# Stores and refills of the images issued by ScalarE instead of GpSimd in a two-layer spectral kernel

## What is computed

```python
# layer 0 (cut)
f = fft2(x, axes=(1, 2)); Xh = f.real - f.imag          # kept: 23 of the width frequencies
o1 = relu(Xk @ w1[0] + b1[0]);  o2 = o1 @ w2[0] + b2[0]
x = ifft2(softshrink(o2, 0.01)).real + x
# layer 1 (cut)
xf = rfft2(x); xr, xi = xf.real, xf.imag
o1r = relu(xr @ w1[0] - xi @ w1[1] + b1[0]);  o1i = relu(xi @ w1[0] + xr @ w1[1] + b1[1])
o2r, o2i = softshrink(...), softshrink(...)
y = irfft2(o2r + 1j * o2i) + x
```

## Time and profile before

| | us |
|---|---|
| median of 3 runs | 584.18 (583.78 to 585.0) |
| the profiled execution | 583.46 |
| its span | 581.6 |
| PE busy in the span | 528.7 (91%) |
| DVE busy | 302.6 (52%) |
| ACT busy | 217.1 (37%) |
| POOL busy | 123.8 (21%) |
| DMA moved | 104.60 MB, mean 180 GB/s |

### The profile page before, as it was taken

How to read it: one execution, slowest core, us unless ns; L and a number is a source line. 1 busy time by engine, 2 the same in 40 slices (tenths; PEclk the granted TensorE clock), 3 DMA queues, 4 the chain that set the end, 5 groups by cost and what they waited for, 6 DMA issues and landing times.

```text
span 581.6 us, 14177 instructions
## 1 busy us (share of the span) xinstructions
PE 528.7 (91%) x5846; PEld 366.4 (63%) x5846; DVE 302.6 (52%) x668; ACT 217.1 (37%) x487; POOL 123.8 (21%) x135
## 2 busy tenths in 40 slices
PE   4308998999999999999999999999999999989787
PEld 1105677667766677667766777667766777776533
DVE  7102444446763476446753576437744576456522
ACT  2203543553334533543345424443245333433102
POOL 9201122001321034111330033102330122011210
PEclk9758999999999999999999999999999999999969
DMA  8795654457894968765885789686885664353486
GB/s 188 216 231 126 167 134 115 129 130 171 243 260 131 200 183 250 225 158 150 258 238 148 163 220 267 183 180 170 252 242 129 155 184 149 89 116 96 132 214 200
DMA packets 76718, 104.60 MB, mean 180 GB/s; under 512 B 7762, under 2 KB 63304, under 8 KB 76527
## 3 DMA queue, kind: packets, MB, share of 16 engines
q1 hardware_dynamic: 61906, 60.14, 39.9%
q0 software_dynamic: 10608, 40.45, 25.5%
q10 hardware_dynamic: 4140, 3.11, 2.4%
HBM read 52.23 MB, written 51.43 MB: 178 GB/s over the span
## 4 chain that ended last, share of the span: by engine, by line
PE 85%; DMA 4%; DVE 4%; issue 3%; SPq 2%; POOL 1%; ACT 1%; POOLq 0%; DVEq 0%; ACTq 0%
PE ps L632 14%; PE ps L656 12%; PE ps L563 12%; PE ps L532 11%; PE ps L580 11%; PE ps L619 10%; PE ps L596 6%; PE ps L643 5%; PE ps L607 3%; DMA scr_f<-fs 3%; PE ps L567 2%; DVE img L511 1%; DMA bt<-scr_f 1%; SPq L257 1%; DVE ns L493 1%
## 5 line engine op out<-in xcount | busy, mean ns | idle before, releaser
L532 PE MATMUL ps<-img,cst 128*64 128x384 f32 (+1 forms) x368 | 82.9, 523 | 16.1 <-ACT fs L369 8.4
L511 DVE TENSOR_TENSOR img<-ps,img 90x768 f32<-90x768 f32 x90 | 81.4, 905 | 26.0 <-PE ps L563 24.7
L563 PE MATMUL ps<-jr,cst 64*128 64x384 f32 (+1 forms) x368 | 83.8, 523 | 5.5 <-DVE img L511 5.0
L341 POOL TENSOR_TENSOR xs<-xs,nt 128x360 f32<-128x360 f32 (+1 forms) x48 | 41.8, 870 | 219.0 <-ACT xs L378 165.1
L632 PE MATMUL ps<-wt,o 128*109 128x96 f32 (+1 forms) x768 | 85.0, 263 | 1.1 <-DVE o L477 0.3
L632 PEld LDWEIGHTS ps<-wt,o 128*109 128x109 f32 (+1 forms) x768 | 76.3, 171 | 14.5 <-issue 10.0
L580 PE MATMUL ps<-cst,bt 128*64 128x90 f32 x1472 | 68.9, 247 | 17.6 <-DMA bt<-scr_f 17.6
L485 DVE SCALAR_TENSOR_TENSOR ns<-p,ps 109x384 f32<-109x384 f32 x96 | 53.1, 553 | 58.5 <-ACT p L403 58.5
L656 PE MATMUL ps<-ns,cst 64*90 64x192 f32 x736 | 73.6, 330 | 7.7 <-DVE ns L493 7.6
L656 PEld LDWEIGHTS ps<-ns,cst 64*90 64x90 f32 x736 | 59.2, 154 | 32.4 <-issue 30.6
L580 PEld LDWEIGHTS ps<-cst,bt 128*64 128x64 f32 x1472 | 60.2, 139 | 29.6 <-DMA bt<-scr_f 18.0
(11 more groups left out here) (41 smaller groups left out, 415.0 us busy)
## 6 DMA issues: line engine op xcount, KB each, us to landing
y<-img POOLq DMA_DIRECT2D x35, 540.0 KB, 5.0
img<-x POOLq DMA_DIRECT2D x30, 540.0 KB, 7.4
scr_i<-et SPq DMA_DIRECT2D x48, 270.0 KB, 3.5
scr_f<-fs SPq DMA_DIRECT2D x176, 72.0 KB, 3.1
bt<-scr_f SPq DMA_DIRECT2D x40, 270.0 KB, 4.7
jr<-scr_i SPq DMA_DIRECT2D x48, 216.0 KB, 6.3
y<-img SPq DMA_DIRECT2D x11, 270.0 KB, 2.9
img<-x SPq DMA_DIRECT2D x5, 540.0 KB, 8.3
```

Source lines behind the costliest of these rows:

```text
L341: nc.gpsimd.tensor_tensor(re, re, nt[s % 2][:, :, 0:kws(s), 0:H], ALU.subtract).then_inc(re_ok, 1)
L511: nc.vector.tensor_tensor(y, p, y, ALU.add).then_inc(i_add, 1)
L532: last = mm(ps[64 * r:64 * r + 64, P3 + g % 2, 0:(b - a) * HC], K["w_fwd"], img[t % IMGS][:, a:b, :].rearrange("p h c -> p (h c)"), start= ...
L563: last = mm(ps[:, B0 + r, 0:n], K["w_inv"][64 * r:64 * r + 64, :], jr[k][64 * r:64 * r + 64, at, 0:n], start=True, stop=whole)
```

## The change

POOL keeps the clearing of buffers at the start and the subtraction. The stores of y, the refills and the first loads of img2 move into ACT's list, at the same places of `schedule()`'s order; there the first loads of img2 stand ahead of the d0 copy of ACT. A refill now follows the store two chunks later instead of one, and the entry at the head of the next task holds the refills of chunks 4 and 5. The waits for the last stores move from POOL to PE's end.

```diff
 # POOL
-            def refill(t, c):
 ...
-                    if s < NXC:
-                        pool.dma_start(img[2][0:W, r0:r1, :], ...).then_inc(x_ld[2][s], 16)
-                if kind == "inv" and what[0] < TASKS - 1 and (what[1] % 2 == 1 or what[1] == GROUPS - 1):
-                    pool.wait_ge(i_add, t * GROUPS + g + 1)
-                    pool.dma_start(out[...], img[k][0:W, r0:r1, :]).then_inc(y_st[k][c], 16)
-                    if c > 0:
-                        refill(t, c - 1)
-                if kind == "load" and what[0] % STEPS == 2 and what[0] // STEPS >= 2:
-                    refill(what[0] // STEPS - 2, NXC - 1)
 # ACT
+            def refill(t, c):
+                    act.wait_ge(y_st[k][c], 16 * (t // IMGS + 1))
+                    act.dma_start(img[k][0:W, r0:r1, :], x[...]).then_inc(x_ld[k][c], 16)
 ...
+                if kind == "d0" and what[0] < NXC:
+                    act.wait_ge(x_clr[2], 1)
+                    act.dma_start(img[2][0:W, r0:r1, :], ...).then_inc(x_ld[2][s], 16)
+                if kind == "inv" and what[0] < TASKS - 1 and (what[1] % 2 == 1 or what[1] == GROUPS - 1):
+                    act.wait_ge(i_add, t * GROUPS + g + 1)
+                    act.dma_start(out[...], img[k][0:W, r0:r1, :]).then_inc(y_st[k][c], 16)
+                    if c > 1:
+                        refill(t, c - 2)
+                if kind == "load" and what[0] % STEPS == 2 and what[0] // STEPS >= 2:
+                    refill(what[0] // STEPS - 2, NXC - 2)
+                    refill(what[0] // STEPS - 2, NXC - 1)
```

More of the change, by code:

```diff
@@ L341, in _ @@
                     nc.gpsimd.tensor_tensor(re, re, nt[s % 2][:, :, 0:kws(s), 0:H], ALU.subtract).then_inc(re_ok, 1)
-                    if s < NXC:
-                        r0, r1 = s * XCH, min(s * XCH + XCH, H)
-                        pool.dma_start(img[2][0:W, r0:r1, :], x[1, r0:r1, :, 0:HC].rearrange("h w c -> w h c")).then_inc(x_ld[2][s], 16)
-                if kind == "inv" and what[0] < TASKS - 1 and (what[1] % 2 == 1 or what[1] == GROUPS - 1):
-                    t, g = what
-                    c, k, (b, f) = g // 2, t % IMGS, divmod(t, HALVES)
-                    r0, r1 = c * XCH, min(c * XCH + XCH, H)
-                    pool.wait_ge(i_add, t * GROUPS + g + 1)
-                    pool.dma_start(out[b, r0:r1, :, f * HC:(f + 1) * HC].rearrange("h w c -> w h c"), img[k][0:W, r0:r1, :]).then_inc(y_st[k][c], 16)
-                    if c > 0:
-                        refill(t, c - 1)
-                if kind == "load" and what[0] % STEPS == 2 and what[0] // STEPS >= 2:
-                    refill(what[0] // STEPS - 2, NXC - 1)
-            for t in range(TASKS - IMGS, TASKS - 1):
-                for c in range(NXC):
-                    pool.wait_ge(y_st[t % IMGS][c], 16 * (t // IMGS + 1))
         @block.scalar
         def _(act):
+            def refill(t, c):
+                k, t1 = t % IMGS, t + IMGS
+                if t1 < TASKS:
+                    r0, r1 = c * XCH, min(c * XCH + XCH, H)
+                    b, f = divmod(t1, HALVES)
+                    act.wait_ge(y_st[k][c], 16 * (t // IMGS + 1))
+                    act.dma_start(img[k][0:W, r0:r1, :], x[b, r0:r1, :, f * HC:(f + 1) * HC].rearrange("h w c -> w h c")).then_inc(x_ld[k][c], 16)
             for kind, *what in order:
@@ L374, in _ @@
                         act.dma_start(img[1][0:W, r0:r1, :], x[0, r0:r1, :, HC:2 * HC].rearrange("h w c -> w h c")).then_inc(x_first[1][c], 16)
+                if kind == "d0" and what[0] < NXC:
+                    s, = what
+                    r0, r1 = s * XCH, min(s * XCH + XCH, H)
+                    act.wait_ge(x_clr[2], 1)
+                    act.dma_start(img[2][0:W, r0:r1, :], x[1, r0:r1, :, 0:HC].rearrange("h w c -> w h c")).then_inc(x_ld[2][s], 16)
+                if kind == "inv" and what[0] < TASKS - 1 and (what[1] % 2 == 1 or what[1] == GROUPS - 1):
+                    t, g = what
+                    c, k, (b, f) = g // 2, t % IMGS, divmod(t, HALVES)
+                    r0, r1 = c * XCH, min(c * XCH + XCH, H)
+                    act.wait_ge(i_add, t * GROUPS + g + 1)
+                    act.dma_start(out[b, r0:r1, :, f * HC:(f + 1) * HC].rearrange("h w c -> w h c"), img[k][0:W, r0:r1, :]).then_inc(y_st[k][c], 16)
+                    if c > 1:
[3 more added lines that the diff above has]
+                    refill(what[0] // STEPS - 2, NXC - 1)
                 if kind == "a":
@@ L660, in _ @@
             pe.wait_ge(i_act, GROUPS // 2)
+            for t in range(TASKS - IMGS, TASKS - 1):
+                for c in range(NXC):
+                    pe.wait_ge(y_st[t % IMGS][c], 16 * (t // IMGS + 1))
     return nc
```

## The result

The changed kernel took 640.74 us (median of 4 runs, 634.39 to 641.82) against 584.59 us for the kernel before, measured beside it: a ratio of 1.094, interval 1.087 to 1.101. It is slower by 56 us; the forecast was 636, in a range of 612 to 658. The profiled execution took 641.36 us, of which 639.6 are span.

What follows compares the result with a forecast made beforehand. PE, busy 91% of the span, was taken as the bound. 19.4 + 2.2 + 1.5 + 23 + 8 - 2 = 52.1 us on 583.46 gave 635.6; median 0.7 higher, 636 us, range 612 to 658.

Steps and rivals of the forecast that it cites:

- Boundary: Between tasks, ACT waits for the last store's landing before its c1 copies, delaying PE's d1: 5 x 4.6 = 23 us.
- Filler 1: After d1 (groups 1, 5, 9), store and refill delay ACT's d0 copy, then PE's e: 18 places, 19.4 us.
- DMA-bound: Rival: the hardware queue's many packets make landings 7.3 us and a pair's second issue 1.3 us, total 660; chance 0.13.
- Task 6 and filler 3: Task 6's groups 1 and 3 cost 2.2 us; after e, chunk 3's store with refill delays d1, 1.5 us.
- Clock: Behind the stop at each of 5 task boundaries PE runs slower for a while: 1.6 us each, 8 us (0 to 10).
- POOL's gain: PE and its weight loads waited 0.7 + 4.3 us for POOL's subtraction; the change wins 2 us of it.
- DMA engines: The moved 40 MB would take 31% of the engines on ACT's queue and not 25.5%; counted as nothing.

Runs made afterwards that it cites:

- the first experiment: The changed kernel with ACT's refills of chunks 4 and 5 moved from the task's first to its second iteration; 606.8 us, ratio 1.039 to the kernel before.

## Why the prediction was right

- **Boundary**: forecast 5 x 4.6 = 23 us; the five stops of PE were 5.86, 4.05, 4.39, 4.39 and 4.96, together 23.7. The sum was worked out for the first of them and gives 4.6; there the landing was 6.6 us and the stop 5.86, so it is right on the mean of the five and not at its own place. The landing was taken as 5.0 us and was 5.7 (median), the third issue as 0.6 and was 0.33. The guess that the store would land sooner than POOL's 6.8, because the refill ahead is older, came true, and what the runs show speaks for its reason: with the refill 4.1 us ahead the median was 6.6 us, and with a second one only 0.5 to 1.8 us ahead it was 8.7. The hardware queue as such isn't quicker: with only the stores on it they landed in 8.1 us.
- **Filler 1**: forecast 19.4 us for 18 places; measured 18.2 (0.45 or 0.46 at group 1, 1.23 at group 5, 0.91 to 2.44 at group 9, and 0.66 and 0.34 in task 5). The sum was right by luck, by two errors that nearly cancel (3.7 us measured for the eight places without a refill where 6.4 were forecast, 14.5 for the ten with one where 13 were). Without a refill I took 0.8 and it was 0.34 to 0.66, because a store's issue is 0.34 us and not 0.47 and the semaphore is nearly free. The refill of chunk 2 took up to 2.05 us to issue. I had 1.3 us for it only in the DMA-bound rival, and it took 1.29 us or more in three of five tasks.
- **Task 6 and filler 3**: 2.2 and 1.5 forecast; 1.6 and 1.2 measured. In filler 3 the copies were to end at 158.24 instead of 157.49 with d1 at 158.10, which makes d1 0.15 to 0.2 us late and not 0.3; it was 0.23 to 0.27.
- **Clock**: forecast 8 us; PE's busy time grew by 15.0. This is the term that was too small. From the start of d1 to the end of the next transpose PE took 7.56, 6.50, 7.90, 6.45 and 6.83 us at the five boundaries, and 4.91 at full clock: 2.65, 1.59, 2.99, 1.54 and 1.92 us, together 10.7. So the 1.6 us that I took from the start of the kernel was right at two boundaries and too small at three. And the step "the stops in filler 1 [...] shouldn't matter" failed for the two longest: behind stops of 2.02 and 2.44 us (at 244.6 and 320.7 us) the granted clock was 0.50, and from the start of e to the start of the next c0 PE took 5.15 and 4.99 us instead of 3.48, 3.2 us more in all. Some 1 us of the 15.0 isn't placed. The runs show both parts: filling the boundaries made the kernel 11 to 15 us faster (3.8 of it in the waits before e), and taking the refills out of filler 1 brought PE busy from 534.9 to 528.7.
- **POOL's gain**: forecast 2 us; the run that moved only the last refill found none, and at most 0.4 us by its interval. The 4.3 us of late weight loads were not on the path.
- **DMA engines**: the hardware queue was to take 22% more engine time for the same bytes. It took 26.6% of 639.6 us for 43.55 MB, 170 us; before, both queues took 27.9% of 581.6 for the same bytes, 162 us: 5% more. The first loads, by which I sized it, ran while the DMA engines were full; that this is the reason is a guess. The rival built on it, DMA-bound, didn't come. The rule of the Trainium skill ("DMA: Bandwidth & Descriptors", the anatomy of one DMA), by which I estimated 2.8 us for the store's landing, is stated there for transfers that GpSimd issues, which I didn't say. It is borne out here neither from GpSimd, where the median was 6.8 us, nor from ACT, where 4.5 us was the shortest.

In all, 52 us were forecast and 56 came. The two main mechanisms and their sizes are as forecast, the clock is nearly twice the forecast, and the gain is missing. The terms as measured, 23.7 + 18.2 + 1.6 + 1.2 + 15.0, make 59.7 us; the spans of the two profiled executions differ by 58.0, as PE's other waits came out some 2 us shorter.

## What to carry to other kernels

A wait costs what stands behind it in the list, not how busy the engine is: the same transfers on ACT cost 56 us or nothing, by their place. Before moving a transfer to an engine that computes for the critical one, look for what it waits for, and put it behind a step for which the engine would wait anyway, with a store's landing at least a step away from the refill that needs it. And a stop of the matmul engine has a second bill, the clock behind it.

## What the runs showed of the hardware

- From POOL the issue of a store or refill took 0.80 to 0.85 us. From ACT 540 KB took 0.33 to 0.73 us at most places of the steps, and up to 2.43 us at others. Among the longest were those of the second refill at the boundary, which follows a store and a refill within 1 us (2.01 to 2.43 us at four of five). But the number of transfers under way doesn't decide it: the refill of chunk 2 in filler 1, always with a refill 5.7 us and a store 0.4 us ahead of it, took 0.53, 1.63, 2.05, 0.91 and 1.29 us in the five tasks. What sets it is open.
- The landing of the same store of 337.5 KB went with what stood around it on its queue. Its medians (seven stores a run) were 4.5 us with a refill 5 to 6 us ahead and none close behind, 5.6 with one behind, 5.7 with two behind, 6.6 with two behind and the one ahead 4.1 us away, and 8.7 with none close behind but one 0.5 to 1.8 us and one 4.1 to 4.3 us ahead. From ACT beside POOL's refills it was 8.1 us.
- Behind a stop of 2.02 and one of 2.44 us, where PE had otherwise hardly stood, the granted clock was 0.50, that is 1.2 GHz; behind stops of 1.29 and 1.67 us at the same place it stayed at 1.00. In the first experiment it was 0.51 behind a stop of 1.87 us and 1.00 behind one of 1.95.
- With stores and refills on ACT's queue, SP's transfers landed sooner: the loads of bt in 3.7 us and not 4.7, the stores of scr_f in 2.2 and not 3.1 (medians). PE had no use for it. No run shows the reason.
